# Two graph attentions: scores from high and low parts, row scaling on GpSimd, half of the copies on VectorE

## The chip, the cores and the metric

One core of one Trainium2 chip runs the whole program. The metric is the device time of one execution in microseconds (us). Engines: TensorE (PE; its weight loads PEld), VectorE (DVE), ScalarE (ACT), GpSimd (POOL), and SyncE (SP), which only issues DMAs here.

## The reference

Four graph layers over 512 nodes of 512 features with 8704 edges, each with a residual sum and a layer norm behind it. Layers 0 and 3 are attentions of 8 heads of 64 features; those are what the change touches.

```python
# layer 0; bias is -1e9 where there is no edge, 0 on the diagonal, the edge's weight where there is one
qkv = x @ Wqkv.T + bqkv
scores = einsum('hnd,hmd->hnm', q, k) / sqrt(64) + bias[None]
attn = softmax(scores, axis=-1)
out = einsum('hnm,hmd->hnd', attn, v)          # then Wo, layer norm, W1, layer norm
# layer 3, by edge: e = k[src] . q[dst] / sqrt(64); softmax over the edges of one dst; sum of attn * v[src];
# then Wo, layer norm, relu(x @ W1 + b1) @ W2 + b2, layer norm
# layers 1 and 2: normalised and typed neighbour sums with dense products
```

The kernel does layer 3 densely as well: an edge that occurs c times adds log c to its score, a pair without an edge gets a mask, and a node without edges is set to 0 by a second factor (`deg[:, 4, i]`).

## The kernel before

Dense products take the operands as a high part (rounded to fp32r) and a low part (the rest) and add three matmuls: low x high, high x low, high x high (`product`, lines 449 to 458). The high parts of evicted tiles are written by ScalarE (`high`), the low parts by VectorE (`low`, a subtraction from PSUM); the low parts of weights by GpSimd (`low(n)`, line 331, four tiles a weight), after `cast(n)` has loaded the high ones.

An attention is 32 items, a head (8) by a tile of 128 query rows (4); item m works on scores of 128 x 512. Pairs of items 2q and 2q+1 are two heads, in partitions 0 to 63 and 64 to 127 of q and k. Before the change q and k are kept in fp32 (`qT`, `kT`), with q scaled by -1/8, and a pair's scores are two fp32 matmuls. An item goes through:

1. TensorE: score matmul into PSUM bank m % 4 (line 545).
2. VectorE: adds the bias and takes the row minimum in one instruction, PSUM to the SBUF tile `sp[m % 6]` (line 1193).
3. ScalarE: exp with the row sum (line 777).
4. VectorE: reciprocal of the sum (line 1200), row scaling (lines 1202, 1204).
5. TensorE: four transposes of 128 x 128 into bank 4 + m % 2 (line 552).
6. ScalarE: copies the transposed row to `probT` (line 785).
7. TensorE: mix with v, head pair by head pair (line 568), into bank 6 or 7.

Every engine takes its instructions in the order in which they are written. Each tile of PSUM is used again only when its bank has been freed (`begin` waits, `frees` counts). TensorE's order at step q: scores of pair q; transposes of items 2q-4 and 2q-3; from step 6 on a quarter of a mix. VectorE's at iteration q: the minima of 2q and 2q+1; reciprocal and scaling of 2q-2 and 2q-1. ScalarE's at item m: exp of m, copy of m-4. The dense products around are: q, k and v ahead; the output product behind. GpSimd, while the first attention runs, works off the low parts of three weights; behind the first attention it adds count tiles (line 384) that VectorE has prepared (`call_halves`).

Of the kernel before, what the change touches and what calls it, by code (L numbers as in the profile page):

```python
# [50 lines left out]
SP = 6  # L51
# [84 lines left out]
def build(nc, x0, x0t, edges, edge_rows, edge_w, weights, rows_of, cols_of, rel_b, ident_d, iota_d, later_d, out):  # L136
# [5 lines left out]
    with ExitStack() as ctx:  # L142
# [14 lines left out]
        def sem(name):  # L157
# [33 lines left out]
        xh = region([("keyb", [P, E + (WINDOW - 1) * P], F32)],  # L191
                    [("counts", [P, 2, 2, T, N], I16), ("x", [P, T, D], F32), ("h", [P, T, D], F32),
                     ("rel_rows", [P, D], F32), ("deg_rows", [P, N], F32)])
        keyb, counts, x, h, rel_rows, deg_rows = (xh[k] for k in ("keyb", "counts", "x", "h", "rel_rows", "deg_rows"))
        y = sb("y", [P, T, D], F32)
# [9 lines left out]
                    [("qT", [P, K, N], F32), ("kT", [P, K, N], F32), ("v", [P, T, D], F32), ("sp", [P, 4, N], F32)])  # L205
# [8 lines left out]
        qT, kT, v = (ab[k] for k in ("qT", "kT", "v"))  # L214
# [15 lines left out]
            "hi_ready", "unpacked", "q_ready", "k_ready", "v_ready", "exped", "scaled",  # L230
# [86 lines left out]
        def _(pool):  # L317
# [13 lines left out]
            def low(n):  # L331
# [4 lines left out]
                for k in range(ks):  # L336
# [11 lines left out]
            pool.memset(nbias[:], MASK).then_inc(s["bias_init"], 1)  # L348
# [72 lines left out]
            pool.wait_ge(ld_par[1], 48)  # L421
            for i in range(T):
                pool.tensor_tensor(y[:, i, :], x[:, i, :], par[:, 1, :], ALU.add).then_inc(s["res_ready"], 1)
# [3 lines left out]
            low(19)  # L427
            cast(20)
            low(20)
# [3 lines left out]
        def _(pe):  # L433
# [101 lines left out]
            def attention(a, base):  # L535
# [3 lines left out]
                for q in range(ITEMS // 2 + 5):  # L539
                    if q < ITEMS // 2:  # L540
                        for m in (2 * q, 2 * q + 1):
                            p, i, e, hd = item(m)
                            rows_ = slice(HD * e, HD * e + HD)
                            begin(("score", a, m))
                            finish(pe.matmul(ps(("score", a, m))[:], qT[rows_, p, i * P:(i + 1) * P], kT[rows_, p, :],  # L545
                                             start=True, stop=True), ("score", a, m))
# [191 lines left out]
        def _(act):  # L738
# [33 lines left out]
            def attention(a, base):  # L772
                for m in range(ITEMS + 4):
# [6 lines left out]
                    if t >= 0:  # L780
# [34 lines left out]
            link(act.activation(cols[:, 0:4], cols[:, 0:4], ACT.Identity, scale=-HD ** -0.5))  # L815
# [19 lines left out]
            for f in range(K):  # L835
                weight_high(7 + f)
                wait_full(act, ("q0", f))
                frees(act.activation(qT[:, f, :], ps(("q0", f))[:], ACT.Identity, bias=cols[:, f:f + 1], scale=-HD ** -0.5), ("q0", f))
            weight_high(11)
            for f in range(K):  # L840
                wait_freed(act, ("q0", f))
                act.sem_inc(s["q_ready"], 1)
            for f in range(K):
                wait_full(act, ("k0", f))
                frees(act.activation(kT[:, f, :], ps(("k0", f))[:], ACT.Identity, bias=cols[:, 4 + f:5 + f]), ("k0", f))
            for f in range(K):
                wait_freed(act, ("k0", f))
                act.sem_inc(s["k_ready"], 1)
# [126 lines left out]
            for f in range(K):  # L975
                wait_full(act, ("k3", f))
                frees(act.copy(kT[:, f, :], ps(("k3", f))[:]), ("k3", f))
            for f in range(K):
                wait_freed(act, ("k3", f))
                act.sem_inc(s["k_ready"], 1)  # L980
# [21 lines left out]
        def _(dve):  # L1002
# [117 lines left out]
            link(dve.tensor_scalar(ewn[:], ew[:], -1.0, None, ALU.mult))  # L1120
# [43 lines left out]
            for b in range(8):  # L1164
# [8 lines left out]
                                         op0=ALU.add, op1=ALU.add).then_inc(s["unpacked"], 1)  # L1173
            dve.wait_ge(ld_par[0], 16)
# [7 lines left out]
            def attention(a, base, mask):  # L1182
                for q in range(ITEMS // 2 + 1):
                    if q == 0:
                        dve.wait_ge(s["bias_loaded" if a == 0 else "bias3_ready"], 16 if a == 0 else T)
                    if q < ITEMS // 2:
                        for m in (2 * q, 2 * q + 1):
                            p, i, e, hd = item(m)
                            c, name = base + m, ("score", a, m)
                            wait_full(dve, name)  # L1190
                            if m >= SP:
                                wait_full(dve, ("probT", a, m - SP))
                            frees(dve.tensor_tensor_reduce(sp[m % SP][:], ps(name)[:], nbias[:, i, :], 1.0, 3e38, ALU.add, ALU.min,  # L1193
                                                           peak[:, c:c + 1]), name)
                    if q >= 1:
                        for t in (2 * q - 2, 2 * q - 1):
# [282 lines left out]
```

## Time and profile before

| | us |
|---|---|
| median of 3 runs | 628.55 |
| lowest, highest | 623.87, 629.28 |
| the profiled execution | 631.25 |
| its span in the profile | 629.5 |

The span is what the profile shows from the first to the last instruction; 1.75 us of the execution lie around it. Busy shares of the engines: TensorE 89%, VectorE 61%, ScalarE 39%, GpSimd 38%. The attentions lie at 178.4 to 235.5 us and at 522.1 to 578.3 us. A busy share tells what an engine did, not whether anyone waited for it; for that there are the chain of waits and the timelines.

### The profile page before, as it was taken

What the parts mean: (1) busy time and instruction counts of PE and PEld (TensorE: products, weight loads), DVE (VectorE), ACT (ScalarE), POOL (GpSimd) and SP (SyncE); (2) the same over time, 40 slices, a digit from 0 to 9 for tenths busy, and PEclk for the clock granted to TensorE, in tenths of its full rate; (3) what the DMA queues carried; (4) which work ended last, traced back from release to release, by engine and by line L of the source; (5) the groups of instructions that cost most, each with busy time, mean ns of one, the idle gap of its engine ahead of it and who ended that gap; (6) DMA issues with size and microseconds to landing.
All of it is one profiled execution on the core that took longest, in us unless ns stands there. A gap on an engine that the chain in (4) does not pass through costs nothing.

```text
span 629.5 us, 7530 instructions
## 1 busy us (share of the span) xinstructions
PE 563.1 (89%) x2433; PEld 355.0 (56%) x2448; DVE 384.2 (61%) x939; ACT 242.9 (39%) x510; POOL 238.4 (38%) x210
## 2 busy tenths in 40 slices
PE   6998999993988999987999899996999998999691
PEld 2443444462843446666767688864877784445560
DVE  7986988993069868967646413134245416884736
ACT  3100700062247864573642221213433116885434
POOL 6565666668554004307213152333152664000000
PEclk8999999997999999997999899997999998999986
DMA  8720000022556000247222142244251844000001
GB/s 275 315 71 2 0 0 0 0 69 79 186 154 180 4 2 0 68 106 179 75 76 86 48 133 68 67 134 125 77 183 52 247 128 126 0 1 2 1 1 67
DMA packets 29383, 53.32 MB, mean 85 GB/s; under 512 B 4945, under 2 KB 6429, under 8 KB 28838
## 3 DMA queue, kind: packets, MB, share of 16 engines
q1 hardware_dynamic: 15436, 26.09, 14.0%
q0 software_dynamic: 11968, 19.96, 11.0%
q10 hardware_dynamic: 1946, 6.85, 3.3%
q8 instruction: 17, 0.28, 0.2%
q14 instruction: 16, 0.13, 0.1%
HBM read 50.73 MB, written 2.17 MB: 84 GB/s over the span
## 4 chain that ended last, share of the span: by engine, by line
PE 67%; DVE 17%; ACT 6%; issue 5%; POOL 2%; DMA 2%; ACTq 0%; DVEq 0%; POOLq 0%
PE bank L478 18%; PE bank L455 11%; PE bank L456 11%; PE bank L457 11%; PE bank L568 4%; PE bank L545 3%; PE bank L552 3%; DVE h L1040 2%; DVE sp L1193 2%; PE bank L447 2%; POOL edge_bias L364 1%; ACT waste L762 1%; ACT gap L762 1%; DVE h L1049 1%; DVE h L1048 1%
## 5 line engine op out<-in xcount | busy, mean ns | idle before, releaser
L341 POOL TENSOR_TENSOR wl<-wraw,wh 128x512 fp32r<-128x512 f32 (+1 forms) x82 | 106.9, 1324 | 98.7 <-DMA wh<-w 33.1
L478 PE MATMUL bank<-hot 128*128 128x512 bf16 x529 | 118.9, 383 | 5.6 <-DVE hot L1097 4.8
L478 PEld LDWEIGHTS bank<-hot 128*128 128x128 bf16 x544 | 53.4, 99 | 70.8 <-DVE hot L1097 6.2
L364 POOL DMA_INDIRECT edge_bias<-ewn,cell_at x68 | 76.5, 1125 | 44.3 <-DVE cell_at L1091 19.1
L455 PE MATMUL bank<-th,wl 128*128 128x512 f32 x104 | 43.4, 417 | 15.0 <-POOL wl L341 12.4
L455 PE MATMUL bank<-wh,tl 128*128 128x512 f32 x112 | 46.2, 412 | 3.0 <-DVE tl L1008 3.0
L457 PE MATMUL bank<-wh,th 128*128 128x512 f32 x112 | 44.4, 397 | 0.0
L456 PE MATMUL bank<-wl,th 128*128 128x512 f32 x112 | 44.4, 397 | 0.0
L456 PE MATMUL bank<-tl,wh 128*128 128x512 f32 x104 | 42.8, 411 | 0.0
L457 PE MATMUL bank<-th,wh 128*128 128x512 f32 x104 | 42.3, 407 | 0.0
L777 ACT ACTIVATE sp<-sp,peak 128x512 f32<-128x512 f32 x44 | 31.7, 720 | 25.7 <-DVE peak L1193 25.4
L1097 DVE TENSOR_SCALAR hot<-iota,pair_dst,digit 128x1024 bf16<-128x1024 f16 x68 | 40.7, 598 | 0.0
L1193 DVE CUSTOM_DVE_ANT_0 sp<-bank,nbias 128x512 f32<-128x512 f32 x44 | 28.4, 686 | 19.2 <-PE bank L545 19.2
L1079 DVE SCALAR_TENSOR_TENSOR eq<-keyb,key,later 128x384 f16<-128x384 f16 (+1 forms) x68 | 39.8, 610 | 0.0
L1096 DVE TENSOR_SCALAR hot<-iota,ef 128x512 bf16<-128x512 f16 x68 | 30.0, 441 | 15.6 <-PE bank L478 14.9
L545 PE MATMUL bank<-kT,qT 64*128 64x512 f32 x128 | 37.6, 651 | 0.8 <-issue 0.8
L785 ACT COPY probT<-bank 128x512 f32<-128x512 f32 x64 | 36.1, 570 | 2.7 <-PE bank L552 2.4
L762 ACT ACTIVATE gap<-h,neg 128x512 f32<-128x512 f32 x24 | 17.3, 721 | 51.2 <-DVE neg L1019 51.2
L552 PEld LDWEIGHTS bank<-ident,sp 128*128 128x128 f32 x176 | 19.3, 144 | 25.9 <-DVE sp L1204 11.4
L568 PE MATMUL bank<-probT,v 128*64 128x512 f32 x128 | 32.8, 612 | 0.0
L455 PEld LDWEIGHTS bank<-th,wl 128*128 128x128 f32 x104 | 20.9, 201 | 21.0 <-POOL wl L341 11.1
L552 PE MATMUL bank<-ident,sp 128*128 128x128 f32 x176 | 26.9, 288 | 5.9 <-ACT probT L785 3.0
(194 smaller groups left out, 1083.2 us busy)
## 6 DMA issues: line engine op xcount, KB each, us to landing
wraw<-w SPq DMA_DIRECT2D x26, 256.0 KB, 2.9
wh<-w POOLq DMA_DIRECT2D x6, 1024.0 KB, 5.8
keyb<-edge_keys ACTq DMA_DIRECT2D x4, 1088.0 KB, 12.0
wh<-w_rel POOLq DMA_DIRECT2D x4, 1024.0 KB, 5.8
wraw<-w_rel SPq DMA_DIRECT2D x16, 256.0 KB, 2.7
wraw<-w_qkv SPq DMA_DIRECT2D x12, 256.0 KB, 6.4
wraw<-w_o SPq DMA_DIRECT2D x8, 256.0 KB, 3.0
wh<-w_o POOLq DMA_DIRECT2D x2, 1024.0 KB, 5.8
```

The source lines that it names most:

```text
L341: pool.tensor_tensor(wl[n % WSLOTS][:, k, 0:width], wraw[:, q % 3, 0:width], wh[n % WSLOTS][:, k, 0:width], ALU.subtract).then_inc(s["w_lo ...
L364: pool.indirect_dma_start(out=bias_dram, out_offset=bass.IndirectOffsetOnAxis(ap=cell_at[:, c:c + 1], axis=0), in_=ewn[:, c:c + 1], in_off ...
L455: pe.matmul(ps(name)[:], al, bh, start=start and k == 0, stop=False)
L456: pe.matmul(ps(name)[:], ah, bl, start=False, stop=False)
L457: mm = pe.matmul(ps(name)[:], ah, bh, start=False, stop=stop and k == ks - 1)
L478: mm = pe.matmul(ps(name)[:], hot[:, slot, 0, i * P:(i + 1) * P], hot[:, slot, 1 + kind, :], start=False, stop=last, skip_group_check=True)
L545: finish(pe.matmul(ps(("score", a, m))[:], qT[rows_, p, i * P:(i + 1) * P], kT[rows_, p, :], start=True, stop=True), ("score", a, m))
L552: mm = pe.transpose(ps(("probT", a, t))[:, j * P:(j + 1) * P], sp[t % SP][:, j * P:(j + 1) * P], ident[:])
L568: mm = pe.matmul(ps(name)[HD * e:HD * e + HD, :], v[:, j, hd * HD:(hd + 1) * HD], probT[:, hd % 4, j, :], start=j == 0, stop=j == T - 1, s ...
L1079: return dve.scalar_tensor_tensor(out=eq[:, k, :], in0=keyb[:, bass.ds(c * P, WINDOW * P)], scalar=key[:, bass.ds(c, 1)], in1=later[:], op ...
L1097: dve.tensor_scalar(hot[:, slot, 1:3, :].rearrange("p a n -> p (a n)"), iota[:], pair_dst[:, bass.ds(j, 1)], digit[:, bass.ds(j, 1)], ALU. ...
L1193: frees(dve.tensor_tensor_reduce(sp[m % SP][:], ps(name)[:], nbias[:, i, :], 1.0, 3e38, ALU.add, ALU.min, peak[:, c:c + 1]), name)
```

## The change

- q and k are evicted as high parts (`qh`, `kh`, ScalarE) and low parts (`ql`, `kl`, VectorE, new helper `part_low`); the scores of a pair become three parts, each of two fp32r matmuls. The scale of -1/8 moves into VectorE's bias and minimum instruction; bias, mask and edge weights are multiplied by 8 and change sign for it.
- Row scaling moves from VectorE to GpSimd: `scale_rows`, one tensor_scalar with two factors for each item, with low parts of weights in between. The residual sums that GpSimd did ahead of an attention are done behind it (`next_residual`), since `kl` lies in the same memory as `y`.
- The copies of even transposed rows stay on ScalarE, those of odd ones go to VectorE, whose order in an iteration is now: minimum of 2q, reciprocals of 2q-2 and 2q-1, minimum of 2q+1, copy of row 2q-5.

```diff
@@ gpsimd @@
+            def scale_rows(a, base, mask, work):
+                for m in range(ITEMS):
+                    p, i, e, hd = item(m)
+                    c = base + m
+                    pool.wait_ge(s["inverse"], c + 1)
+                    pool.tensor_scalar(sp[m % SP][:], sp[m % SP][:], scale[:, c:c + 1], 1.0 if mask is None else mask(i), ALU.mult, ALU.mult)\
+                        .then_inc(s["scaled"], 1)
+                    if m in work:
+                        low(*work[m])
+            def next_residual(a, slot):
+                wait_full(pool, ("score", a, ITEMS - 1))
+                for i in range(T):
+                    pool.tensor_tensor(y[:, i, :], x[:, i, :], par[:, slot, :], ALU.add).then_inc(s["res_ready"], 1)
...
             low(2)
+            cast(3)
+            low(3)
+            cast(4)
+            cast(5)
+            scale_rows(0, 0, None, {4 + 3 * j: (n, [f]) for j, (n, f) in enumerate((n, f) for n in (4, 5) for f in range(K))})
             pool.wait_ge(s["ld_x"], 16)
             pool.wait_ge(ld_par[1], 16)
-            pool.wait_ge(s["x_low"], K)
-            for i in range(T):
-                pool.tensor_tensor(y[:, i, :], x[:, i, :], par[:, 1, :], ALU.add).then_inc(s["res_ready"], 1)
-            for n in (3, 4, 5):
-                cast(n)
-                low(n)
+            next_residual(0, 1)
...
@@ tensor, attention @@
-                        for m in (2 * q, 2 * q + 1):
...
-                            finish(pe.matmul(ps(("score", a, m))[:], qT[rows_, p, i * P:(i + 1) * P], kT[rows_, p, :],
-                                             start=True, stop=True), ("score", a, m))
+                        for part, (left, right) in enumerate(((ql, kh), (qh, kl), (qh, kh))):
+                            for m in (2 * q, 2 * q + 1):
+                                p, i, e, hd = item(m)
+                                rows_ = slice(HD * e, HD * e + HD)
+                                if part == 0:
+                                    begin(("score", a, m))
+                                mm = pe.matmul(ps(("score", a, m))[:], left[rows_, p, i * P:(i + 1) * P], right[rows_, p, :],
+                                               start=part == 0, stop=part == 2)
+                                if part == 2:
+                                    finish(mm, ("score", a, m))
@@ scalar, attention @@
-                    if t >= 0:
+                    if t >= 0 and t % 2 == 0:
@@ scalar, third layer, k (first layer alike, for q and k) @@
-                wait_full(act, ("k3", f))
-                frees(act.copy(kT[:, f, :], ps(("k3", f))[:]), ("k3", f))
+                high(("q3", f), qh[:, f, :], s["q_high"])
             for f in range(K):
+                high(("k3", f), kh[:, f, :], s["k_high2"])
@@ vector @@
+            def part_low(name, f, dst, top, add, highs, done):
+                dve.wait_ge(highs, f + 1 if name[-1] == "0" else K + f + 1)
+                frees(dve.scalar_tensor_tensor(out=dst[:, f, :], in0=ps((name, f))[:], scalar=add, in1=top[:, f, :], op0=ALU.add,
+                                               op1=ALU.subtract), (name, f))
+                wait_freed(dve, (name, f))
+                dve.sem_inc(done, 1)
...
+                def peak_of(m):
+                    name, c = ("score", a, m), base + m
+                    wait_full(dve, name)
+                    if m >= SP:
+                        wait_full(dve, ("probT", a, m - SP))
+                    frees(dve.tensor_tensor_reduce(sp[m % SP][:], ps(name)[:], nbias[:, item(m)[1], :], -HD ** -0.5, 3e38, ALU.add, ALU.min,
+                                                   peak[:, c:c + 1]), name)
+                def inverse_of(t):
+                    c = base + t
+                    dve.wait_ge(s["exped"], c + 1)
+                    dve.reciprocal(scale[:, c:c + 1], total[:, c:c + 1]).then_inc(s["inverse"], 1)
+                for q in range(ITEMS // 2 + 3):
                     if q < ITEMS // 2:
+                        peak_of(2 * q)
+                    if 1 <= q <= ITEMS // 2:
+                        inverse_of(2 * q - 2)
+                        inverse_of(2 * q - 1)
+                    if q < ITEMS // 2:
+                        peak_of(2 * q + 1)
+                    t = 2 * q - 5
+                    if t >= 0:
+                        p, i, e, hd = item(t)
+                        if hd >= 4:
+                            wait_full(dve, ("mix", a, p - 2))
+                        wait_full(dve, ("probT", a, t))
+                        frees(dve.tensor_copy(probT[:, hd % 4, :, i * P:(i + 1) * P],
+                                              ps(("probT", a, t))[:].rearrange("p (j n) -> p j n", j=T)), ("probT", a, t))
                     if q >= 11 and (q - 11) % T == 0:
                         mixed(a, (q - 11) // T)
```

In layer 3 GpSimd's order changes in the same way: `scale_rows(3, ...)` stands behind `cast(20)`, with the low parts of weights 19 and 20 in between its items, and the residual sum behind it.

## Rows read from the trace of the kernel before

**Rows 1.** the page, busy time and share of the span of each engine.

```profile
PE 563.1 (89%) x2433; PEld 355.0 (56%) x2448; DVE 384.2 (61%) x939; ACT 242.9 (39%) x510; POOL 238.4 (38%) x210
```

**Rows 2.** windows of the attentions: stretch, its length, busy us (instructions) by engine.

```profile
178.40:194.70 16.30, 11.95 (x58) 5.64 (x57) 15.37 (x43) 11.05 (x29) 7.63 (x7) 1.00 0.73 199
194.70:224.00 29.30, 28.80 (x147) 12.19 (x146) 25.25 (x76) 23.26 (x58) 5.36 (x4) 1.00 0.18 55
224.00:235.50 11.50, 10.93 (x57) 4.61 (x57) 7.37 (x19) 6.98 (x15) 0.77 (x1) 1.00 0.01 2
522.00:538.00 16.00, 13.10 (x56) 6.54 (x56) 13.71 (x41) 12.26 (x28) 6.43 (x7) 0.89 0.39 105
538.00:566.70 28.70, 28.25 (x147) 12.20 (x146) 24.02 (x76) 23.34 (x59) 0.00 (x0) 1.00 0.00 1
```

**Rows 3.** chain of waits, first attention: start us, us, what.

```profile
207.13 1.01 PE bank L568 x4
208.14 1.07 PE bank L545 x3
...
215.76 1.02 PE bank L552 x8
...
223.98 1.07 PE bank L545 x3
```

**Rows 4.** timeline of TensorE: start us, us, engine, line, what; idle before it, releaser.

```profile
208.07 1.13 PE L545 MATMUL bank<-kT,qT 64*128 64x512 f32 x4
209.13 0.66 PE L552 MATMUL bank<-ident,rel_rows 128*128 128x128 f32 x4
...
213.07 0.63 PE L552 MATMUL bank<-ident,sp 128*128 128x128 f32 x4 [0.19 <-ACT probT L785]
213.63 1.08 PE L568 MATMUL bank<-probT,v 128*64 128x512 f32 x4
```

**Rows 5.** timeline of VectorE in the same step.

```profile
209.23 0.69 DVE L1193 CUSTOM_DVE_ANT_0 sp<-bank,nbias 128x512 f32<-128x512 f32 x1 [0.67 <-PE bank L545]
...
209.85 0.69 DVE L1193 CUSTOM_DVE_ANT_0 sp<-bank,nbias 128x512 f32<-128x512 f32 x1
...
210.46 0.16 DVE L1200 RECIPROCAL scale<-total 128x1 f32<-128x1 f32 x1
210.66 0.49 DVE L1202 TENSOR_SCALAR sp<-sp,scale 128x512 f32<-128x512 f32 x1
```

**Rows 6.** instructions of lines 1140 and 977: duration ns min/median/max, first and last start.

```profile
L1140 DVE COPY packed<-bank x4: 680/681/692, 66.9 to 68.7; 128x512 f32<-128x512 f32 x4
...
L977 ACT COPY kT<-bank x4: 585/587/589, 513.2 to 521.3; 128x512 f32<-128x512 f32 x4
```

**Rows 7.** TensorE in a dense product (timeline), and the matmuls of line 680.

```profile
169.71 0.39 PE L456 MATMUL bank<-wl,th 128*128 128x512 f32 x1
169.94 0.39 PE L457 MATMUL bank<-wh,th 128*128 128x512 f32 x1
...
L680 PE MATMUL bank<-rel_rows,deg_rows x8: 590/592/592, 411.0 to 414.0; 128*128 128x512 f32 x8
```

**Rows 8.** GpSimd's groups by line and shape: count, busy us, mean ns, idle before.

```profile
L341 POOL TENSOR_TENSOR wl<-wraw,wh 128x512 fp32r<-128x512 f32 x78 | 104.0, 1354 | 94.3 <-DMA wh<-w 29.4 <-issue 10.3 <-DMA wh<-w_o 10.3
...
L351 POOL TENSOR_SCALAR_AFFINE_SELECT nbias<-nbias 128x512 f32<-128x512 f32 x4 | 2.5, 616 | 0.3
```

**Rows 9.** timeline of VectorE while GpSimd subtracts (185.29 to 190.60).

```profile
187.37 0.68 DVE L1193 CUSTOM_DVE_ANT_0 sp<-bank,nbias 128x512 f32<-128x512 f32 x1
...
188.17 1.31 DVE L1202 TENSOR_SCALAR rel_rows<-rel_rows,scale 128x512 f32<-128x512 f32 x1
```

**Rows 10.** windows (column after POOL is the granted clock), and TensorE's timeline.

```profile
186.00:190.00 4.00, 2.30 (x14) 1.14 (x12) 3.93 (x9) 3.01 (x8) 4.00 (x4) 1.00 0.46 121
525.00:528.00 3.00, 1.79 (x8) 1.00 (x6) 2.93 (x9) 1.97 (x6) 2.28 (x4) 0.85 0.42 105
...
527.00 1.93 PE L552 MATMUL bank<-ident,sp 128*128 128x128 f32 x8 [1.21 <-DVE sp L1204]
```

More of the change, by code:

```diff
@@ L329, in cast, with low @@
                 pool.dma_start(wh[n % WSLOTS][:, 0:ks, 0:width], weights[name].rearrange("(k p) d -> p k d", p=P)).then_inc(s[f"cast{n % 2}"], 16)
-            def low(n):
+            def low(n, parts=None):
                 _, ks, width = WEIGHTS[n]
@@ L335, in low @@
                     pool.wait_ge(s[f"cast{n % 2}"], 16 * (n // 2 - (0 if n % 2 else 1)))
-                for k in range(ks):
+                for k in range(ks) if parts is None else parts:
                     q = QUARTERS.index((n, k))
@@ L426, in _ @@
             cast(19)
-            low(19)
             cast(20)
-            low(20)
+            scale_rows(3, ITEMS, lambda i: deg[:, 4, i:i + 1],
+                       {4 + 3 * j: (n, [f]) for j, (n, f) in enumerate([(19, 0), (19, 1), (19, 2), (19, 3), (20, 0), (20, 1)])})
+            pool.wait_ge(ld_par[1], 48)
+            next_residual(3, 1)
         @block.tensor
@@ L837, in _ @@
                 wait_full(act, ("q0", f))
-                frees(act.activation(qT[:, f, :], ps(("q0", f))[:], ACT.Identity, bias=cols[:, f:f + 1], scale=-HD ** -0.5), ("q0", f))
+                act.activation(qh[:, f, :], ps(("q0", f))[:], ACT.Identity, bias=cols[:, f:f + 1]).then_inc(s["q_high"], 1)
             weight_high(11)
             for f in range(K):
-                wait_freed(act, ("q0", f))
-                act.sem_inc(s["q_ready"], 1)
-            for f in range(K):
                 wait_full(act, ("k0", f))
[L845 to L848, printed above, removed]
+                act.activation(kh[:, f, :], ps(("k0", f))[:], ACT.Identity, bias=cols[:, 4 + f:5 + f]).then_inc(s["k_high2"], 1)
             attention(0, 0)
@@ L1173, in _ @@
                                          op0=ALU.add, op1=ALU.add).then_inc(s["unpacked"], 1)
+            def part_low(name, f, dst, top, add, highs, done):
[4 more added lines that the diff above has]
+                dve.sem_inc(done, 1)
+            dve.wait_ge(s["ld_cols"], 16)
+            for f in range(K):
+                part_low("q0", f, ql, qh, cols[:, f:f + 1], s["q_high"], s["q_ready"])
+            for f in range(K):
+                part_low("k0", f, kl, kh, cols[:, 4 + f:5 + f], s["k_high2"], s["k_ready"])
             dve.wait_ge(ld_par[0], 16)
@@ L1180, in _ @@
                 dve.sem_inc(s["v_ready"], 1)
[L1182 to L1185, printed above, removed]
-                    if q < ITEMS // 2:
[L1187 to L1196, printed above, removed]
-                            p, i, e, hd = item(t)
-                            c = base + t
-                            dve.wait_ge(s["exped"], c + 1)
-                            link(dve.reciprocal(scale[:, c:c + 1], total[:, c:c + 1]))
-                            if mask is None:
-                                ins = dve.tensor_scalar(sp[t % SP][:], sp[t % SP][:], scale[:, c:c + 1], None, ALU.mult)
-                            else:
-                                ins = dve.tensor_scalar(sp[t % SP][:], sp[t % SP][:], scale[:, c:c + 1], mask(i), ALU.mult, ALU.mult)
-                            ins.then_inc(s["scaled"], 1)
@@ L1389, in _ @@
             for f in range(K):
-                wait_full(dve, ("q3", f))
-                frees(dve.tensor_scalar(qT[:, f, :], ps(("q3", f))[:], -HD ** -0.5, None, ALU.mult), ("q3", f))
-                wait_freed(dve, ("q3", f))
-                dve.sem_inc(s["q_ready"], 1)
-            attention(3, ITEMS, lambda i: deg[:, 4, i:i + 1])
+                part_low("q3", f, ql, qh, 0.0, s["q_high"], s["q_ready"])
+            for f in range(K):
+                part_low("k3", f, kl, kh, 0.0, s["k_high2"], s["k_ready"])
+            attention(3, ITEMS)
             dve.wait_ge(ld_par[2], 48)
```

37 lines of the change are left out of this document (16 added, 21 removed).

## Prediction

> **What bounds the kernel now.** I read the page first: TensorE is busy 89% of the span, VectorE 61%, ScalarE 39%, GpSimd 38% [rows 1]. That is an average, and the change touches two stages, the two attentions, so I cut the span at the score matmuls. Call S(q) the start of the scores of pair q (items 2q and 2q+1). The windows show three parts in each attention: the fill S(0) to S(6), 16.3 us in the first (178.4 to 194.7) and 16.0 in the second; the steady part S(6) to S(15), 29.3 and 28.7 us; and a tail of 11.5 us [rows 2]. In the steady part TensorE is busy 28.8 of 29.3 us and VectorE 25.3; in the fill it is VectorE, 15.4 of 16.3.
>
> The chain of waits says the same and gives the period. In the steady part it runs along TensorE: 1.06 us for the scores of a pair, 1.02 for eight transposes, 1.01 for four records of the mix, then the next scores; the pieces make 3.1 us [rows 3]. Over nine steps it is (223.98 - 194.70) / 9 = 3.25 us [rows 2, 3], because once in four steps the ScalarE eviction of a mix pushes an exp and a copy late and a transpose waits for it [rows 4]. I count those hitches as 0.1 to 0.15 us a step.
>
> **The loop that decides.** The part of the change that looks smallest matters most: which engine copies the odd transposed rows, and where that copy stands. Follow the code at TensorE's step q: scores of 2q and 2q+1, transpose of 2q-4, transpose of 2q-3, a quarter of the mix. The odd transposes share one PSUM bank, so transpose 2q-3 waits until row 2q-5 has been copied out. Before, ScalarE copies 2q-5 behind exp(2q-1), which belongs to the step before; it is normally ready. After, VectorE copies 2q-5 in its iteration q *behind* peak_of(2q+1), and that peak needs the scores that TensorE has just made in step q. So within one step everything is in series: scores q, peak 2q, two reciprocals, peak 2q+1, copy 2q-5, transpose 2q-3, mix, and only then scores q+1. The even transpose alone fits into the wait. Nothing runs ahead, since TensorE is in order and its scores stand behind the waiting transpose. Queued behind the waiting transpose are thus the mix and the next scores; all three other engines wait for those.
>
> **The terms of that loop.**
> - Scores. Before, the two items of a pair lie in different rows of the array and run at once: four records take 1.06 us (208.07 to 209.13), two passes of 0.53 [rows 4]. Single fp32 matmuls over the whole array take 3.0 / 7 = 0.43 us a record (L680), so running two at once costs a factor 1.24. An fp32r matmul of 512 columns goes at 0.23 us [rows 7]. Three parts, each an fp32r pair: no row shows one. Bounds: 0.227 us each (two for the price of one) and 0.454 (one behind the other). I take 0.227 x 1.24 = 0.28, since the fp32 pair is the nearest row. The peak then starts 2 x 0.28 + 0.39 (the length of an fp32r record [rows 7]) + 0.03 (209.20 to 209.23 [rows 4, 5]) = 0.98 us behind S.
> - Peak to peak on VectorE 0.62 and 0.61 [rows 5]. The two reciprocals between them: 0.16 us each by the record, partly overlapping, 0.1 to 0.3; I take 0.2.
> - Copy of 512 columns from PSUM on VectorE: 0.68 (L1140) [rows 6], and 0.1 to TensorE's start.
> - Four transposes to the mix: 213.63 - 213.07 = 0.56 [rows 4]. Four mix records 1.01 [rows 3].
>
> Sum: 0.98 + 0.62 + 0.20 + 0.61 + 0.68 + 0.10 + 0.56 + 1.01 = 4.76 us a step with a mix, 3.75 without one.
>
> **The steps of the change and what each costs.**
> - Steady part: 9 x 4.76 = 42.8 us against 29.3 and 28.7: +13.5 and +14.1.
> - Fill: scores 0 to 2 are not yet in the loop; S(3) falls at about 5.0 us, by the latency of peak, exp, reciprocal, scaling and transpose. Then three steps of 3.75: S(6) at 16.2. Before it was 16.3 and 16.0. So the lighter VectorE gains nothing there that the loop doesn't take back; +0.3 for the second attention, +0 for the first.
> - Tail: step 15 is a full step, transposes 28 to 31 each follow a copy. By the same terms the last mix ends 12.8 us behind S(15) instead of 11.5 (224.0 to 235.5): +1.3 twice.
> - Head: q and k are now evicted twice, high part on ScalarE, low on VectorE. In the first attention v's product covers it. In the second the last k tile was ready for TensorE one ScalarE copy (0.59) after its product [rows 6]; now a VectorE subtraction from PSUM of about 0.7 us follows: +0.7. The cover is gone there because nothing else is queued on TensorE.
> - Scaling moves to GpSimd, one instruction an item. No row shows GpSimd's tensor_scalar; the nearest are an affine select with one input, 0.62 us, and a subtraction with two, 1.35 mean [rows 8]. I take 0.65, one SBUF input. A step then asks 2 x 0.65 and two thirds of a weight subtraction (1.3 x 2/3 = 0.87), 2.2 us of 4.76; even at 1.35 it asks 3.6. Hidden in the steady part; at 1.35 the fill gets about 1 us longer in each attention, which I keep for the range.
> - VectorE loses 64 scalings: 0.49 us each [rows 5], 1.31 when GpSimd was at a subtraction [rows 9]. That time is no longer on the path, as VectorE waits for TensorE. Its remaining operations read PSUM, and a peak beside GpSimd's subtraction kept its 0.68 [rows 9].
> - ScalarE loses 32 copies, off the path: free.
> - On GpSimd's queue, weight subtraction 3 and the loads 3 to 5 move ahead of the scaling, the residual sum behind it (four sums of two inputs like the subtractions, 1.35 each, 5.4 in all [rows 8]). The last scaling ends some 4.4 us behind S(15), so the sums end before the tail's 12.8 us are over, before call_halves needs GpSimd. The load of slot 5 waits for the v product, which ends as attention starts, and the first scaling is needed 3 us later: free. SyncE's raw loads are released by the subtractions and come later, for weights used tens of us on. Mask and sign edits replace one instruction by another of the same shape; one small ScalarE instruction goes.
>
> A rule of the skill bears on the last engine change. The row shows a VectorE scaling at 1.31 instead of 0.49 us beside GpSimd's subtraction [rows 5, 9]. The Trainium skill, SBUF — State Buffer, "rules for kernel authors", says that VectorE in a two-port mode and GpSimd lock each other out for whole instructions. By that, taking the scaling off VectorE removes the lock; by the loop above the time it frees is idle. The Trainium skill, GPSIMD Engine Reference, section 3.1, gives an estimate of 0.77 us for a tight one-input loop over 512 elements; the sum would be the same by it, since it hides as well.
>
> **The sum.** 13.5 + 14.1 + 0.3 + 2.6 + 0.7 = 31.2 us. The profiled execution took 631.25 us with a span of 629.5; the median of three runs is 628.55, 2.7 lower. I add the sum to the median: 659.7 us, and expect a span near 660.7.
>
> **Rivals.**
> - *Score pairs don't overlap in fp32r.* Then six matmuls at 0.227 stand in a row and the peak starts 4 x 0.227 + 0.42 = 1.33 behind S instead of 0.98: +0.35 in 15 steps, twice: 670. For it: six weight loads instead of four a pair, each before its matmul. Against: the fp32 pair does overlap.
> - *The clock falls.* In the loop TensorE has 2.9 of 4.8 us to do, 60%. One stretch with 2.30 busy of 4.00 kept the full 2.4 GHz; in another, with 1.79 busy of 3.00, it had begun to fall (mean 0.85), and eight transposes took 1.93 us [rows 10], near twice their 1.02, as at 1.2 GHz. With all of TensorE's path doubled a step would be about 2.2 us longer (scores 0.7 to 0.85, one transpose group 0.5, mix 0.9). If a third of 24 steps ran so: +17, 677.
> - *Faster: the odd copy does not hold TensorE.* If the copy were ready when transpose 2q-3 comes, TensorE would bound as before with 0.84 + 1.02 + 1.01 = 2.87 us a step instead of 3.2: 2 x 9 x 0.35 = 6.3, and 2 us of the fill: 620. It decides if copy 2q-5 ends within 0.5 us of the scores' end; the code puts at least 1.9 us of VectorE work between (0.62 + 0.61 + 0.68). For it speaks only that busy times alone (VectorE 2.1, GpSimd 2.2) stay under TensorE's.
> - *GpSimd bounds.* A scaling above (4.76 - 0.87) / 2 = 1.95 us would. Both nearest rows are far below: at 2.3 us it adds 0.7 a step, 17 in 24 steps, 677.
>
> **How the numbers follow.** Forecast 0.67, pairs in series 0.13, clock 0.09, faster 0.05, GpSimd 0.03, and 0.03 for a gain elsewhere that makes it no change. The forecast's own range: parts at 0.227 instead of 0.28, reciprocals at 0.1 and copy at 0.60 take 0.29 from each of 24 steps, 7 us; a slower GpSimd and waits of 0.1 more a step add 4: 652 to 665. Eight in ten must take in the pairs in series and the clock partly: 650 to 675. A measurement here can tell about 1% from no change. Faster by over 1%: 0.05; within 1%: 0.03; slower: 0.92.
>
> **What the profile after would show.** Steps of 4.6 to 4.9 us between score groups in the steady part; TensorE idle about 1.7 us ahead of every odd group of transposes, released by VectorE's copy; that copy right behind the odd peak; VectorE idle until TensorE's scores; the fill's length unchanged; GpSimd's scaling 0.6 to 0.8 us. I am wrong if TensorE's waits before transposes name another releaser, or if the steps stay near 3 us.

## The result and the profile after

| | before | changed |
|---|---|---|
| median of 5 runs, us | 627.16 | 665.68 |
| lowest, highest | 623.83, 629.28 | 660.07, 666.62 |
| profiled execution | 631.25 | 660.07 |
| its span | 629.5 | 658.3 |

The ratio is 1.0604, with an interval from 1.0549 to 1.0659: slower by 6%. Ratios leave out executions over 1.5% longer than the fastest of their kernel. The forecast was 659.7 us, 650 to 675, and 660.7 for the span. As a slowdown it was 31.2 us; the two medians are 38.5 us apart, the spans of the two profiled executions 28.8.

The page's busy times (before: [rows 1]) give TensorE nearly the same work over a longer span, VectorE and ScalarE a little less, GpSimd more:

```profile
PE 560.4 (85%) x2497; PEld 360.3 (55%) x2512; DVE 375.3 (57%) x919; ACT 230.2 (35%) x481; POOL 282.9 (43%) x274
```

The windows of the attentions, cut as in [rows 2] at the start of the scores, at S(6), at S(15) and at the end of the last mix; behind POOL's column stands the granted clock:

```profile
175.40:192.10 16.70, 11.01 (x71) 6.75 (x70) 11.11 (x38) 10.94 (x28) 10.03 (x13) 1.00 0.42 125
192.10:234.80 42.70, 28.05 (x164) 13.65 (x164) 18.90 (x64) 18.98 (x47) 19.68 (x24) 1.00 0.13 38
234.80:248.70 13.90, 12.27 (x61) 5.48 (x59) 7.78 (x18) 3.76 (x8) 8.50 (x9) 0.88 0.00 0
...
550.50:593.20 42.70, 28.04 (x165) 13.63 (x164) 18.90 (x64) 18.97 (x47) 17.51 (x22) 1.00 0.02 7
```

The steady part takes 42.7 us in both attentions, where it took 29.3 and 28.7. TensorE is busy 28.05 of 42.7 us in it, VectorE 18.9: no engine is full any more, which is how a loop of waits looks. The fills last 16.7 us (16.6 in the second attention), the tails 13.9 (14.0).

The chain of waits through one step, to be read beside [rows 3]:

```profile
200.58 1.01 PE bank L590 x4
201.58 0.90 PE bank L565 x6
202.49 0.60 PE bank L574 x4
...
203.13 0.08 DVE peak L1217
203.21 0.14 DVE scale L1224 x2
203.35 0.59 DVE deg_rows L1217
...
203.94 0.61 DVE probT L1240
...
204.69 0.63 PE bank L574 x4
205.32 1.01 PE bank L590 x4
```

Before, three TensorE pieces stood in the chain. Now it goes from the scores into VectorE: the first minimum (the chain shows its read-out), two reciprocals, the second minimum, the copy (L1240), and back into the odd transposes. The even transposes (202.49) stand in the chain only because they run beside the first minimum; that minimum waits for the scores and not for them, as VectorE's timeline below shows. The step is 205.32 - 200.58 = 4.74 us. The timelines of TensorE and VectorE in that step have the terms (before: [rows 4, 5]):

```profile
199.95 0.63 PE L574 MATMUL bank<-ident,deg_rows 128*128 128x128 f32 x4 [1.63 <-DVE probT L1240]
...
201.51 0.51 PE L565 MATMUL bank<-kh,ql 64*128 64x512 f32 x2
...
202.42 0.65 PE L574 MATMUL bank<-ident,sp 128*128 128x128 f32 x4
...
204.69 0.52 PE L574 MATMUL bank<-ident,sp 128*128 128x128 f32 x3 [1.62 <-DVE probT L1240]
```

```profile
202.51 0.69 DVE L1217 CUSTOM_DVE_ANT_0 rel_rows<-bank,nbias 128x512 f32<-128x512 f32 x1 [2.71 <-PE bank L565]
...
203.13 0.22 DVE L1224 RECIPROCAL scale<-total 128x1 f32<-128x1 f32 x2
203.27 0.67 DVE L1217 CUSTOM_DVE_ANT_0 deg_rows<-bank,nbias 128x512 f32<-128x512 f32 x1
...
203.86 0.69 DVE L1240 COPY probT<-bank 128x512 f32<-128x512 f32 x1
```

TensorE stood idle 1.62 us until VectorE's copy, VectorE 2.71 us until TensorE's scores: each waits for the other in turn. In the first attention up to 235 us the waits are, by who waited for whom (us, times, longest):

```profile
PE bank L574 <- DVE probT L1240: 19.5, 12, 1.6
...
DVE sp L1217 <- PE bank L565: 17.1, 9, 2.7
```

GpSimd's scaling, with the constant 1.0 and with a column as second factor (ns min/median/max):

```profile
L356 POOL TENSOR_SCALAR sp<-sp,scale x22: 679/692/695, 178.7 to 239.2; 128x512 f32<-128x512 f32 x22
L356 POOL TENSOR_SCALAR sp<-sp,scale,deg x22: 755/767/777, 537.1 to 597.7; 128x512 f32<-128x512 f32 x22
```

Where the 28.8 us of the two spans lie, from the starts of the scores and the ends of the mixes: ahead of the first attention -3.0 (175.4 instead of 178.4), first attention 73.3 instead of 57.2, between the attentions 285.2 instead of 286.5, second attention 73.3 instead of 56.3, behind it nothing. The -3.0 need not be the change's: in the traces below, with the same work ahead, the first scores start anywhere from 174.5 to 181.4 us, some 24 us behind the start of the load that follows the scatter of the edge weights (150.7 to 156.8). The stretch between the attentions varies as well, from 282.8 to 291.9 us. So where traces are compared below, the lengths of the attentions themselves tell more than the spans.

### The profile page after: what moved, and what is told of

The parts are those of the page before. It is cut to its first block, busy times and chain, and to the rows that moved or that the text cites. A ratio compares the mean times of both kernels' runs of the same rounds, so it can differ in the third digit from the quotient of the medians.

```text
span 658.3 us, 7684 instructions
## 1 busy us (share of the span) xinstructions
PE 560.4 (85%) x2497; PEld 360.3 (55%) x2512; DVE 375.3 (57%) x919; ACT 230.2 (35%) x481; POOL 282.9 (43%) x274
## 4 chain that ended last, share of the span: by engine, by line
PE 69%; DVE 19%; ACT 4%; issue 4%; POOL 2%; DMA 2%; ACTq 0%; DVEq 0%; POOLq 0%
PE bank L496 17%; PE bank L473 11%; PE bank L474 10%; PE bank L475 10%; PE bank L574 6%; PE bank L590 4%; PE bank L565 4%; DVE probT L1240 2%; DVE sp L1217 2%; PE bank L465 2%; DVE h L1053 2%; POOL edge_bias L383 1%; PE bank L542 1%; ACT gap L784 1%; ACT waste L784 1%
## 5 line engine op out<-in xcount | busy, mean ns | idle before, releaser
L574 PE MATMUL bank<-ident,sp 128*128 128x128 f32 x176 | 28.8, 289 | 30.6 <-DVE probT L1240 29.2
L1110 DVE TENSOR_SCALAR hot<-iota,pair_dst,digit 128x1024 bf16<-128x1024 f16 x68 | 43.4, 638 | 0.0
L574 PEld LDWEIGHTS bank<-ident,sp 128*128 128x128 f32 x176 | 19.0, 144 | 44.0 <-POOL rel_rows L356 18.3
L474 PE MATMUL bank<-tl,wh 128*128 128x512 f32 x104 | 42.8, 411 | 0.0
L1109 DVE TENSOR_SCALAR hot<-iota,ef 128x512 bf16<-128x512 f16 x68 | 28.8, 423 | 11.6 <-PE bank L496 9.8
L590 PE MATMUL bank<-probT,v 128*64 128x512 f32 x128 | 34.8, 642 | 0.0
L473 PEld LDWEIGHTS bank<-wh,tl 128*128 128x128 f32 x112 | 21.3, 190 | 17.3 <-issue 13.4
L1021 DVE TENSOR_TENSOR tl<-bank,th 128x512 fp32r<-128x512 f32 x32 | 21.7, 684 | 12.0 <-ACT th L774 7.4
```

Source lines behind the costliest of these rows:

```text
L473: pe.matmul(ps(name)[:], al, bh, start=start and k == 0, stop=False)
L474: pe.matmul(ps(name)[:], ah, bl, start=False, stop=False)
L574: mm = pe.transpose(ps(("probT", a, t))[:, j * P:(j + 1) * P], sp[t % SP][:, j * P:(j + 1) * P], ident[:])
L590: mm = pe.matmul(ps(name)[HD * e:HD * e + HD, :], v[:, j, hd * HD:(hd + 1) * HD], probT[:, hd % 4, j, :], start=j == 0, stop=j == T - 1, s ...
L1110: dve.tensor_scalar(hot[:, slot, 1:3, :].rearrange("p a n -> p (a n)"), iota[:], pair_dst[:, bass.ds(j, 1)], digit[:, bass.ds(j, 1)], ALU. ...
```

## The experiments

Compare ratios rather than times: the kernel before took 626.5 us beside the first four kernels (copy first, copy in the middle, copies on ScalarE, changed kernel again), 631.0 beside the next four (filled wait, scores alone, copies alone, fp32 scores) and 627.9 or 628.1 beside the last four.

**The order of the copy.** First the step that the forecast rests on. Two kernels keep the whole change and only put one copy elsewhere; a third gives it to ScalarE. The first, with the copy ahead of the minima:

```diff
                 for q in range(ITEMS // 2 + 3):
+                    t = 2 * q - 5
+                    if t >= 0:
+                        ...
+                        frees(dve.tensor_copy(probT[...], ps(("probT", a, t))[...]), ("probT", a, t))
                     if q < ITEMS // 2:
                         peak_of(2 * q)
...
-                    t = 2 * q - 5
-                    ...
```

> The changed kernel, with VectorE's copy of row 2q-5 moved to the head of its iteration q, ahead of the minimum of 2q; nothing else. Series theory (the copy holds the odd transpose, and so the next scores): the copy is ready before transpose 2q-3 comes, steps fall from 4.75 to 2.9 to 3.2 us bound by TensorE, each attention gets about 21 us shorter: 616 to 624 us, under the kernel before. Rival (the dearer parts are the scores in three parts and the scaling on GpSimd, and their latency takes the copy's place): steps stay above 4.2 us, 645 us or more. VectorE's idle time before the minima shrinks by the first theory and stays by the second.

617.20 us, ratio 0.9857 (0.9823 to 0.9891). TensorE's timeline:

```profile
192.94 1.08 PE L590 MATMUL bank<-probT,v 128*64 128x512 f32 x4
...
194.85 1.09 PE L574 MATMUL bank<-ident,sp 128*128 128x128 f32 x8
195.87 1.08 PE L590 MATMUL bank<-probT,v 128*64 128x512 f32 x4
```

The eight transposes stand in one piece of 1.09 us, with no wait in front of the odd four, and a step takes 195.87 - 192.94 = 2.93 us. Moving one instruction ahead of four others took the ratio from 1.0604 to 0.9857, 7%. It follows that neither the three parts of the scores nor GpSimd's scaling held the loop of 4.74 us.

With the copy between the minimum of 2q and the reciprocals:

> The changed kernel, with the copy of row 2q-5 between the minimum of 2q and the two reciprocals. Series theory: the two reciprocals and one minimum, about 0.75 us, leave the loop of every step: 4.0 us a step, 24 steps: 18 us less than the changed kernel, 645 to 649. Rival (any order that lets VectorE start the copy early is as good as another, or none is): the same time as with the copy first, or as the changed kernel.

642.03 us, ratio 1.0258 (1.0216 to 1.0299). The transposes of two steps:

```profile
199.21 0.63 PE L574 MATMUL bank<-ident,sp 128*128 128x128 f32 x4 [0.89 <-DVE probT L1235]
...
203.23 0.63 PE L574 MATMUL bank<-ident,sp 128*128 128x128 f32 x4 [0.90 <-DVE probT L1235]
```

4.02 us a step. Taking two reciprocals and a minimum (0.14 + 0.61 us) out of the loop takes 0.73 off the step. The ratio fell by 3.3 to 4.1% against the two measurements of the changed kernel, 21 to 27 us, more than the 18 expected, and the median lies below the 645 to 649. Its mean clock was 0.960 to 0.963; the next group of experiments takes that up.

With all copies on ScalarE (`if t >= 0`, and no copy on VectorE):

> The changed kernel with all copies on ScalarE again; scores in three parts and scaling on GpSimd are kept. Series theory: as with the copy first, 616 to 626 us, since ScalarE has 2.4 us of work a step of 2.9 to 3.2. Rival (GpSimd's scaling or the scores cost the time): 645 us or more.

617.59 us, ratio 0.9866 (0.9828 to 0.9905), the same as with the copy first. Which engine copies did not matter here, as both get there in time.

The same part alone in the kernel before, behind both scalings of VectorE's iteration:

```diff
@@ scalar @@
-                    if t >= 0:
+                    if t >= 0 and t % 2 == 0:
@@ vector, end of iteration q, behind the scalings of 2q-2 and 2q-1 (and two more iterations) @@
+                    t = 2 * q - 5
+                    if t >= 0:
+                        ...
+                        frees(dve.tensor_copy(probT[...], ps(("probT", a, t))[...]), ("probT", a, t))
```

> The kernel before with one part of the change: odd rows copied by VectorE, at the end of its iteration, behind both minima and both scalings; fp32 scores, scaling on VectorE. Series theory: the loop is now 1.16 to the minimum, 1.23 for two, 1.3 for two reciprocals and scalings, 0.8 for the copy, 0.56 and 1.01: 6.0 us a step with a mix, 5.0 without: 18 x 2.8 and 6 x 2 and a longer tail, 60 to 70 us slower, 686 to 698. Rival (moving a copy of 0.6 us from one engine with room to another costs little): within 10 us of 626.

737.68 us, ratio 1.1746 (1.1667 to 1.1825), well over the expectation. The chain of waits:

```profile
234.47 0.89 PE bank L552 x4
235.35 1.91 PE bank L568 x4
...
242.03 1.09 PE bank L552 x4
...
249.36 0.63 PE bank L552 x4
249.99 1.01 PE bank L568 x4
251.00 1.07 PE bank L545 x3
...
255.34 1.09 PE bank L552 x4
```

The step that starts at the full clock (mix 1.01, scores 1.07) runs from 249.36 to 255.34: 5.98 us, the 6.0 of the expectation. The one before, with a mix of 1.91 us, took 242.03 - 234.47 = 7.56. So the step was sized right at the full clock, and what I had left out is the clock at least: it averages 0.74 and 0.84 over the two attentions. How much of the 40 us beyond the expectation it explains, no run separates.

**The clock.** The profiled run of the changed kernel was the fastest of its five (mean granted clock 0.961, the others 0.945 to 0.956).

> The changed kernel once more, for a second trace and more times. Its profiled run took 660.1 us with a mean clock of 0.961, the other runs 664.8 to 666.6 with 0.945 to 0.956. If the difference is TensorE's clock in the loop, a run near 665 shows more stretches at 1.2 GHz inside the attentions than the 2 of the first trace (one in each tail). If it is the scatter of the edge weights ahead of the first attention, attention 1 starts 3 us or more later and the attentions are as long as before.

668.09 us, ratio 1.0697 (1.0645 to 1.0749). Windows of its first attention:

```profile
175.00:189.10 14.10, 10.06 (x64) 6.17 (x64) 9.31 (x32) 8.94 (x23) 8.67 (x11) 1.00 0.48 145
189.10:199.30 10.20, 7.61 (x27) 3.85 (x27) 3.84 (x14) 4.00 (x10) 3.96 (x5) 0.50 0.14 51
```

From 189.1 to 199.3 us the granted clock was 0.50, 1.2 of 2.4 GHz; ahead of it TensorE had been busy 10.06 of 14.10 us. Four shorter stretches followed in the attentions. First to last score took 64.1 and 64.4 us here and 59.9 and 59.8 in the first trace; that trace had its stretches in the tails (clock 0.88 there), which cost 1.6 us each (14.0 us a tail against 12.4 here). The first scores started at 175.1 us, against 175.4, so the scatter is not the reason. The two attentions together take 152.2 us here and 146.6 in the first trace; the difference of 5.6 is the whole difference of the spans (664.0 and 658.3).

Is it the want of work that lets the clock fall? This kernel gives TensorE more work, in the wait:

```diff
                             begin(("probT", a, t))
-                            for j in range(T):
-                                mm = pe.transpose(...)
+                            for again in range(3 if t % 2 == 0 and 2 <= t < 28 else 1):
+                                for j in range(T):
+                                    mm = pe.transpose(...)
                             finish(mm, ("probT", a, t))
```

> The changed kernel, with the four transposes of every even row 2 to 26 done three times over into the same place (the result is the same): TensorE gets 1.02 us more work in each wait of 1.6 us, and the loop stays as it is. If the excess of the typical runs over the first trace is TensorE's clock, which falls for want of work in the loop, the stretches at 1.2 GHz inside the attentions go and the median falls from 666 or 668 to 658 to 662, although TensorE does more. Rival (the excess has to do with the scatter or the memory): the median stays at 665 to 668.

662.86 us, but on a set of runs where the kernel before took 630.98: ratio 1.0525 (1.0476 to 1.0575), against 1.0604 and 1.0697 for the changed kernel. Its timeline and window:

```profile
205.12 1.53 PE L575 MATMUL bank<-ident,sp 128*128 128x128 f32 x12
207.41 0.63 PE L575 MATMUL bank<-ident,sp 128*128 128x128 f32 x4 [0.76 <-DVE probT L1241]
...
212.15 0.63 PE L575 MATMUL bank<-ident,sp 128*128 128x128 f32 x4 [0.76 <-DVE probT L1241]
```

```profile
178.10:238.00 59.90, 50.04 (x331) 31.31 (x332) 30.03 (x102) 30.57 (x75) 29.67 (x37) 1.00 0.23 69
```

Twelve transposes where four stood, the wait shorter (0.76 us), the step unchanged (212.15 - 207.41 = 4.74), and the clock at 1.00 over the whole attention; all its runs had a mean clock of 0.962 or more. Work that nobody needs made the kernel 0.7 to 1.6% faster by the ratios. Against the first measurement the intervals overlap, against the second they don't, and the median lies between the 658 to 662 of the expectation and the 665 of its rival. The traces are plainer: the two attentions take 143.4 us here, 146.6 in the first trace of the changed kernel and 152.2 in the second. The clock's share of those two is thus 3 and 9 us.

**The other parts.** fp32 scores in the changed kernel (q and k evicted once, by ScalarE):

> The changed kernel with fp32 scores again (q and k evicted once, by ScalarE); order, scaling and copies stay changed. The minimum of 2q starts 1.16 us behind the scores' start in the trace before and 1.00 in the one after: 0.16 more in 30 steps, 5 us, less 0.7 ahead of the second attention: 669 to 673, with the same clock. If the scores in three parts were a cost, it would be below 662.

666.51 us, ratio 1.0583 (1.0529 to 1.0637): by the ratios not 5 us dearer than the changed kernel (1.0604, 1.0697), rather cheaper. The loop did what was expected:

```profile
206.59 0.69 DVE L1213 CUSTOM_DVE_ANT_0 rel_rows<-bank,nbias 128x512 f32<-128x512 f32 x1 [2.87 <-PE bank L564]
...
211.50 0.69 DVE L1213 CUSTOM_DVE_ANT_0 sp<-bank,nbias 128x512 f32<-128x512 f32 x1 [2.87 <-PE bank L564]
```

211.50 - 206.59 = 4.91 us a step, 0.17 more than with the parts. At an equal clock the traces show the price as well: the second attention, at 1.00 throughout, takes 74.1 us, each of the filled wait's, at 1.00 too, 71.7. That is 2.4 an attention, 5 for both, as expected. The ratios hide it because the mean clock was 0.956 to 0.961 here, where the changed kernel had 0.945 to 0.961 and then 0.939 to 0.949. It fits that shorter scores leave TensorE more idle in a loop in which it waits anyway, and that the clock falls more often for it; but the kernels were measured at different times, and no run shows it.

The scores in parts alone, in the kernel before (the odd copies back on ScalarE, scaling back on VectorE in its order of before):

> The kernel before with one part of the change: scores in three fp32r parts (q and k evicted twice, the scale in the minimum, the residual sums behind the attention); scaling on VectorE in the order of before, all copies on ScalarE. A pair's scores took 0.90 us in the trace after and 1.06 before: 0.16 off each of the 18 steady steps, 3 us less, 0.7 more ahead of the second attention: 622 to 626, against 626.5. Rival (the three parts are what makes the series kernel slow): over 635.

632.44 us, ratio 1.0034 (1.0001 to 1.0067): a miss, 0.3% slower instead of 0.5% faster. The same with more work in the fill:

```diff
+                            for again in range(2 if t < 10 else 1):
-                            for j in range(T):
+                                for j in range(T):
                                     ...
```

> The kernel with the scores in parts alone, with the transposes of rows 0 to 9 of each attention done twice into the same place (the result is the same): 1.02 us more for TensorE in each of five steps of the fill, where it waits 1.2 us a step for VectorE. The trace with the parts alone had 13.7 us at 1.2 GHz there (185 to 199), the one before none. If the clock ate the 3 us that the shorter scores give, the stretch goes and the ratio to before falls from 1.003 to 0.993 to 0.998. Rival (the parts cost elsewhere, ahead of the attentions or on VectorE): the ratio stays at 1.003 or rises, since TensorE has 10 us more to do.

626.35 us, ratio 0.9985 (0.9960 to 1.0009). The window from 185 to 199 us, first of the parts alone, then with the work added:

```profile
185.00:199.00 14.00, 12.41 (x48) 7.91 (x50) 13.35 (x33) 8.75 (x22) 7.09 (x6) 0.51 0.48 151
```

```profile
185.00:199.00 14.00, 12.27 (x90) 8.53 (x86) 13.01 (x35) 10.73 (x28) 5.72 (x5) 1.00 0.36 100
```

0.51 and 1.00 in the clock's column. The stretch went with the added work, and the ratio fell by 0.5%, a little less than expected, and the two intervals touch.

Yet the traces do not show that the clock made the miss. With the parts alone the two attentions take 58.6 and 55.8 us, with the work added and without the stretch 58.8 and 56.1, and in the kernel before 57.2 and 56.3. The scores did give what they should: the steady parts are 2.0 and 1.0 us shorter than before (27.2 and 27.6 instead of 29.2 and 28.7). But both tails take 12.6 us instead of 11.7, and the first fill 18.8 (18.3 with the work added) instead of 16.3. There VectorE scales beside GpSimd, whose order this kernel has changed. Its residual sums now start with the last score, and TensorE waits 0.47 and 0.76 us for the two scalings beside them:

```profile
227.11 5.34 POOL L362 TENSOR_TENSOR y<-x,par 128x512 f32<-128x512 f32 x4 [33.24 <-PE bank L562]
```

```profile
228.36 1.55 DVE L1224 TENSOR_SCALAR rel_rows<-rel_rows,scale 128x512 f32<-128x512 f32 x1
...
230.02 1.30 DVE L1224 TENSOR_SCALAR deg_rows<-deg_rows,scale 128x512 f32<-128x512 f32 x1
```

Such a scaling takes 0.49 us alone. In the first fill five of them take 1.30 to 1.59 us beside the weight subtractions, where before there were three. So the kernel with the parts alone carries a second change, and by the traces it is this one that ate the gain. No run takes it out, so that the parts alone make the kernel faster is not shown.

The scaling back on VectorE, in the kernel with the copy first:

```diff
@@ gpsimd @@
-                    pool.tensor_scalar(sp[m % SP][:], ...)
@@ vector, inverse_of @@
                     dve.reciprocal(scale[:, c:c + 1], total[:, c:c + 1]).then_inc(s["inverse"], 1)
+                    dve.wait_ge(s["inverse"], c + 1)
+                    dve.tensor_scalar(sp[t % SP][:], sp[t % SP][:], scale[:, c:c + 1], ...)
```

> The kernel with the copy first, with the scaling back on VectorE. VectorE then has 0.69 + 2 x 0.61 + 2 x 0.65 = 3.2 us a step against TensorE's 2.9 and becomes the bound, in the fill too: 24 to 30 steps by 0.3 and more in the fill: 8 to 14 us over the copy first, ratio to before 1.00 to 1.01. If the scaling on GpSimd brought nothing, the ratio stays 0.986.

638.27 us, ratio 1.0146 (1.0072 to 1.0219): 2.9% over the copy first, more than expected. Windows of the first attention: fill, steady part (S(6) to S(15)) and tail:

```profile
178.81:197.76 18.95, 14.16 (x69) 8.55 (x69) 18.21 (x43) 9.29 (x24) 11.28 (x9) 0.73 0.62 177
197.76:226.43 28.67, 27.32 (x163) 13.68 (x162) 27.98 (x85) 20.40 (x49) 0.00 (x0) 1.00 0.00 1
226.43:239.74 13.31, 10.92 (x61) 4.93 (x59) 11.40 (x25) 5.27 (x12) 6.23 (x5) 1.00 0.01 2
```

```profile
185.74 1.61 DVE L1224 TENSOR_SCALAR sp<-sp,scale 128x512 f32<-128x512 f32 x1
...
187.46 1.30 DVE L1224 TENSOR_SCALAR sp<-sp,scale 128x512 f32<-128x512 f32 x1
```

VectorE is full in fill and steady part (18.21 of 18.95, 27.98 of 28.67). With the copy first and the scaling on GpSimd the three parts take 12.4, 27.2 and 11.0 us. Over both attentions the scaling on VectorE costs 21.6 us: 4.1 in the steady parts, where I had expected 5.4, 11.3 in the fills and 6.2 in the tails. In the fill stand scalings of 1.61 and 1.30 us beside GpSimd's subtractions and a clock of 0.73, in the tail a scaling of 1.30 beside its residual sums. The edit has also taken GpSimd's wait for the reciprocals away, so that all its subtractions fall into the fill (11.28 us there, 0.00 in the steady part). So in the steady parts the scaling on GpSimd is worth 4 us. Most of the 2.9% lies where VectorE would scale beside GpSimd's two-input work, and where the clock fell too; no run separates the two.

Copy first with fp32 scores:

> The kernel with the copy first, with fp32 scores. Steps bound by TensorE, 1.06 + 1.02 + 1.01 = 3.09 instead of 2.92 us: 18 x 0.17 = 3 us more, less 0.7 ahead of the second attention and whatever of the fill is bound by others: ratio to before 0.988 to 0.992. If the clock decides here as it did in the series kernel, the mean clock is no higher than with the copy first (0.958 to 0.963), since TensorE is busy in both; if the parts cost clock here too, it is higher and the ratio is 0.986 or less.

621.20 us, ratio 0.9893 (0.9831 to 0.9955). As expected in size (0.4% over the copy first), though the intervals overlap, and with the copy first's mean clock (0.956 to 0.962 in four of its five executions, 0.952 in the fifth, of 630.87 us, against 0.958 to 0.963): where TensorE was busy anyway, the parts cost no clock.

The last is an attempt at the best version: `{5 + 2 * j: ...}` instead of `{4 + 3 * j: ...}` in both calls of `scale_rows`.

> The kernel with the copy first, with GpSimd's weight subtractions always behind an odd item instead of behind every third. In the trace with the copy first, the chain goes through a subtraction of 1.25 us that stands between the scalings of one pair and holds the odd transpose some 0.2 to 0.7 us. If these holds count, 1 to 3 us less than with the copy first: ratio to before 0.980 to 0.985. If the next wait takes their place, the same ratio, 0.986.

617.22 us, ratio 0.9834 (0.9789 to 0.9879) against 0.9857 (0.9823 to 0.9891): not told apart by the times. The traces do tell: the attentions take 49.8 and 49.2 us instead of 50.6 and 50.1, all at a clock of 1.00, 1.7 us less together, within the 1 to 3 expected. Both kernels beat the one before by 1.4 to 1.7%, with intervals that leave out 1.

## Why the prediction was right

- *The loop* was right in its order, its releaser and its size: 4.76 us forecast, 4.74 measured, and 42.8 against 42.7 for the nine steps. By terms: start of scores to minimum 0.98, measured 1.00 (201.51 to 202.51); minima 0.62 and 0.61, measured 0.62 and 0.59; reciprocals 0.20, measured 0.14; copy with its way to TensorE 0.78, measured 0.83; transposes and mix 1.57, measured 1.56 (199.95 to 201.51). With the copy first, in the middle, and behind the scalings of the kernel before, the step followed its place each time: 2.93, 4.02, 5.98 us.
- *Scores.* 0.28 us a part was the value between 0.227 and 0.454; three parts take 0.90. The rival of pairs in series is out. But the factor of 1.24 behind the 0.28 was a misreading, and that the 0.98 came out is partly luck. The three parts of the step above start at 201.51, 201.85 and 202.08 and the transposes at 202.42: 0.34, 0.23 and 0.34 us. Where two pairs' scores stand in a row, the parts follow each other every 0.22 to 0.24 us, the time of one matmul of 128 rows [rows 7], so running two at once costs nothing, and what is added is about 0.1 us at each end of the scores. The second attention's first scores show it:

```profile
534.20 0.43 PE L565 MATMUL bank<-kl,qh 64*128 64x512 f32 x2
534.42 0.43 PE L565 MATMUL bank<-kh,qh 64*128 64x512 f32 x2
534.66 0.42 PE L565 MATMUL bank<-kh,ql 64*128 64x512 f32 x2
```

- *Fill.* 16.2 forecast, 16.7 and 16.6 measured.
- *Tail.* +1.3 each forecast, +2.4 and +2.4 measured; 1.6 of that is the clock (the mix took 1.90 and 1.91 us instead of 1.01 once in each tail).
- *Head of the second attention.* +0.7 forecast; TensorE's gap ahead of the scores is 1.50 us instead of 0.77.
- *GpSimd's scaling.* 0.65 assumed, 0.69 and 0.77 measured, hidden in the steady part as forecast. That VectorE's freed time would bring nothing held in this kernel; with the copy first the move brings 2.9%. The Trainium skill, SBUF — State Buffer, "rules for kernel authors", says that of a VectorE instruction in a two-port mode and a GpSimd instruction, the one that comes second waits until the first has ended. The traces agree as far as they go: the minima beside GpSimd's instructions kept 0.69 us, the scaling on VectorE went from 0.49 to 1.30 and up to 1.61. In which mode it runs, no trace shows.
- *The sum* fell short in one term, the clock. I gave it a chance of 0.09 as a rival, for a third of the steps; in fact it is part of the result. For fills, steady parts and tails I forecast 30.5 us. At a clock of 1.00 (the filled wait) the two attentions take 143.4 us against 113.4 before, 30.0 more; in the two traces of the changed kernel they take 33.1 and 38.8 more. The forecast slowdown missed that of the medians by 7 us (31.2 and 38.5). Executions between the two traces, nearer to the second, would account for it, and the mean clocks fit that: 0.961 and 0.946 in the traces, 0.945 to 0.956 in the other four executions of the first measurement.
- *The span* was nearly hit, 658.3 where I said 660.7, by terms that cancel, which is luck: the first attention started 3.0 us early and the stretch between the attentions was 2.0 shorter than forecast, while the attentions took 2.6 more.
- *The rows were there:* 1.79 busy of 3.00 us went with a falling clock [rows 10], and I weighed the one stretch that kept it as much as the one that did not. The range held the time because it reached towards this rival.

## What to carry to other kernels

When work moves to another engine, its place in that engine's order counts for more than its cost: write down, for one step, which instruction each wait needs and what stands ahead of that on its engine, and look for a way that leads from an engine back to itself within the step. Where an in-order engine frees a buffer that an earlier engine needs, put the freeing instruction ahead of those that need fresh input. A loop of waits on TensorE can cost twice: its idle time (30 us here), and a lower granted clock for the work that is left (3 and 9 us in the two traces). And when one part of a change is tried alone, look in the trace at what else has moved with it: here GpSimd's sums had come to lie beside VectorE's scaling.

## What the runs showed of the hardware

- Two fp32r matmuls of 64 rows and 512 columns in different halves of the array, pair after pair, take 0.23 us a pair, as one of 128 rows does. In fp32 a pass of such a pair takes 0.43 us (starts at 178.95 and 179.38 in the trace before), as one of 128 rows does. About 0.1 us is added at each change between the scores and the matmuls of 128 rows around them.
- Transposes that are done over again kept TensorE's clock at 2.4 GHz over both attentions (71.7 us each, against 73.3 and 73.3, 75.9 and 76.3 without them), at no cost to the step of 4.74 us.
- GpSimd's tensor_scalar of 128x512 fp32 takes 0.69 us with a constant as second factor and 0.77 with a column, a good half of its two-input subtraction (1.31 mean).
- VectorE's tensor_scalar of 128x512 fp32 takes 0.49 us alone and 1.30 to 1.61 beside a two-input instruction of GpSimd; its minimum, which reads PSUM, keeps 0.69.
